# A tuned AdaLN attention block: new instruction orders on VectorE, ScalarE and GpSimd, weight pieces split in twos

## The reference, cut to what matters

```python
# x: 4 batches of 512 tokens, 512 wide; 32 query heads, 8 key/value heads, head width 128
h = layernorm(x) * (1 + ca) + sa
q = rope(h @ Wq.T)                               # 32 heads
c_kv = h @ Wdk.T
k = rope half of (h @ Wkr.T), other half (c_kv @ Wupk.T)
v = c_kv @ Wupv.T                                # 8 heads, each used by 4 query heads
p = softmax(causal(q @ k.T / sqrt(128)))
x = x + ga * ((p @ v) @ Wo.T)
h = layernorm(x) * (1 + cb) + sb
w = top-8 of softmax(h @ router.T + bias), others 0     # 64 experts
x = x + gb * (h * sum(w) + w @ expert_bias)
```

## Time and profile before

| | |
|---|---|
| Median of 3 runs | 1593.63 us (1592.9 to 1594.1) |
| The profiled execution's own time | 1594.98 us |
| Its span, first to last instruction | 1593.7 us |
| Busy: TensorE / VectorE / GpSimd / ScalarE | 93% / 74% / 67% / 61% |
| Granted TensorE clock, mean | 0.989 |

### The profile page before, as it was taken

One profiled execution on the slowest core, in us unless ns is written; L12 is line 12 of the kernel. 1 busy time (PEld: TensorE's weight loads), 2 busy tenths in 40 slices (PEclk: granted clock), 3 DMA queues, 4 the chain that ended last, 5 costly groups with the idle time before them and its releaser, 6 DMA issues.

```text
span 1593.7 us, 24295 instructions
## 1 busy us (share of the span) xinstructions
PE 1487.0 (93%) x7096; PEld 1223.8 (77%) x7096; DVE 1174.3 (74%) x3441; ACT 979.3 (61%) x2317; POOL 1063.5 (67%) x827
## 2 busy tenths in 40 slices
PE   7978999999999999999999999999899998899986
PEld 5567888888888888887888888888777777778864
DVE  6866777777777777777777777777787887788856
ACT  3256666666766666666667666666565555556663
POOL 1757766676665676666666567665676877786765
PEclk9999999999999999999999999999999999999997
DMA  8555665665765666566476566667687778677760
GB/s 306 204 177 178 220 189 178 183 202 174 208 205 169 196 202 192 181 195 198 160 216 200 166 206 203 193 187 225 190 245 219 253 219 261 217 234 253 235 215 27
DMA packets 210980, 321.99 MB, mean 202 GB/s; under 512 B 38416, under 2 KB 128272, under 8 KB 210848
## 3 DMA queue, kind: packets, MB, share of 16 engines
q1 hardware_dynamic: 210528, 320.33, 63.8%
q10 hardware_dynamic: 320, 0.11, 0.0%
HBM read 179.42 MB, written 140.94 MB: 201 GB/s over the span
## 4 chain that ended last, share of the span: by engine, by line
PE 45%; POOL 29%; DVE 10%; issue 5%; ACT 5%; DMA 4%; SPq 2%; DVEq 0%; POOLq 0%; ACTq 0%
PE bank_s L513 13%; POOL PT_lo L1551 13%; PE bank_o L613 10%; PE bank_pv L595 9%; PE bank_s L562 7%; PE bank_s L536 4%; DMA PT_raw<-blocks 3%; POOL qT_lo L1544 3%; POOL rot_c L1539 2%; POOL kT_lo L1560 2%; POOL kv_raw L1556 2%; ACT PT_hi L902 1%; DVE rot_s L1168 1%; DVE OT_lo L1231 1%; DVE rot_s L1169 1%
## 5 line engine op out<-in xcount | busy, mean ns | idle before, releaser
L1551 POOL TENSOR_TENSOR PT_lo<-PT_raw,PT_hi 128x640 fp32r<-128x640 f32 x252 | 393.7, 1586 | 47.5 <-ACT PT_hi L902 47.5
L888 ACT ACTIVATE probs<-probs,row_inv 128x512 f32<-128x512 f32 (+3 forms) x512 | 259.2, 555 | 252.2 <-DVE row_inv L1206 249.2
L1539 POOL TENSOR_TENSOR rot_c<-rot_c,rot_s 128x512 f32<-128x512 f32 x128 | 166.2, 1298 | 366.7 <-DVE rot_s L1169 366.5
L881 ACT ACTIVATE probs<-probs,row_min 128x512 f32<-128x512 f32 (+3 forms) x512 | 281.6, 552 | 120.8 <-DVE row_min L1200 120.8
L1200 DVE CUSTOM_DVE_ANT_0 probs<-bank_s,mask 128x512 f32<-128x512 f32 (+3 forms) x512 | 226.8, 487 | 2.3 <-issue 0.9
L562 PE MATMUL bank_s<-kT_lo,qT_hi 128*128 128x512 f32 (+3 forms) x512 | 165.2, 323 | 54.7 <-DVE kv_rot L1178 36.0
L1223 DVE STREAM_TRANSPOSE blocks<-probs 128x384 f32<-128x384 f32 x508 | 211.3, 445 | 3.6 <-POOL hT_lo L1529 2.1
L513 PE MATMUL bank_s<-hT_lo,wq_hi 128*128 128x512 f32 x500 | 201.5, 403 | 2.1 <-DVE row_min L1200 0.8
L613 PE MATMUL bank_o<-wo_lo,OT_hi 128*128 128x512 f32 x504 | 196.8, 391 | 2.9 <-DVE OT_lo L1231 2.9
L1544 POOL TENSOR_TENSOR qT_lo<-rot_c,qT_hi 128x512 fp32r<-128x512 f32 x128 | 167.3, 1307 | 46.8 <-ACT qT_hi L863 46.8
L613 PE MATMUL bank_o<-wo_hi,OT_lo 128*128 128x512 f32 x504 | 196.8, 390 | 0.0
(11 more groups left out here) (252 smaller groups left out, 3352.3 us busy)
## 6 DMA issues: line engine op xcount, KB each, us to landing
blocks<-blocks SPq DMA_DIRECT2D x127, 640.0 KB, 2.9
PT_raw<-blocks SPq DMA_DIRECT2D x504, 160.0 KB, 3.7
stage<-in_wq SPq DMA_DIRECT2D x32, 256.0 KB, 4.4
vblocks<-kv_raw SPq DMA_DIRECT2D x32, 256.0 KB, 4.0
kv_raw<-vblocks SPq DMA_DIRECT2D x128, 64.0 KB, 2.0
stage<-in_wo SPq DMA_DIRECT2D x32, 256.0 KB, 3.4
split_wq<-wq_hi SPq DMA_DIRECT2D x32, 256.0 KB, 4.1
split_wq<-wq_lo SPq DMA_DIRECT2D x32, 256.0 KB, 4.7
```

The costliest lines, as they stand in the source:

```text
L881: ins = act.activation(row(t, qt), row(t, qt), ACT.Exp, bias=row_min[m][:, qt:qt + 1], scale=-1.0, accum_out=row_sum[m][:, qt:qt + 1])
L888: ins = act.activation(row(t, qt), row(t, qt), ACT.Copy, scale=row_inv[t % 2][:, qt:qt + 1])
L1539: pool.tensor_tensor(rot_c[:], rot_c[:], rot_s[:], ALU.add).then_inc(pool_a, 1)
L1551: pool.tensor_tensor(lo[:, at], raw_of(t)[:, at], hi[:, at].bitcast(F32), ALU.subtract).then_inc(pool_t, 1)
```

## The change

**VectorE**: in h1 the low part of the values (`v_split_lo`) moves from behind `q_rope` and the second `invert_sums` to between the first `invert_sums` and `q_rope`. **ScalarE**: in h1 the high part of the values moves ahead of the second half of the exponentials; in h2 the high part of the keys moves from between the exponentials to between the two halves of `normalise`; the high part of the query made in an even step moves from that step's end to the next odd step's start, behind `pair_split_hi`. **GpSimd**: the low part of the query made in an even step moves likewise to the start of the odd step; the key's rotation moves from the end of h1 to h2, behind the low part of the probabilities, and the key's low part from before `q_rope` in h2 to after it; the FFN's pieces move (`ffn_gate` of a tile from two steps before its use to the start of the odd step in which VectorE uses it, `ffn_out` from the even step's end to the odd step's start). **Weights**: two pieces are split in every second step, in even steps only, and the order of the pieces changes; SyncE's loads and stores of them move into odd steps, and its store of a finished FFN tile (`store_out`) from the even step to the odd step. No instruction is added or removed.

```diff
--- before.py
+++ after.py
@@ -36,10 +36,11 @@
 LOWEST = -3e38
 
 
-CHUNKS = ["wo0", "wo1", "wo2", "wo3", "wk", "wq0", "wv", "wq1", "wq2", "wq3"]
-CHUNK_STEP = {1: [0], 2: [1], 3: [2], 4: [3], 5: [4], 6: [5], 7: [6], 8: [7], 9: [8], 10: [9]}
+CHUNKS = ["wo0", "wo1", "wo2", "wo3", "wk", "wq0", "wq1", "wq2", "wv", "wq3"]
+CHUNK_STEP = {2: [0, 1], 4: [2, 3], 6: [4, 5], 8: [6, 7], 10: [8, 9]}
 HALVES = [(3, 2), (1, 0)]
-FIRST_CHUNKS = CHUNKS[4:]
+
+FIRST_CHUNKS = ["wk", "wq0", "wv", "wq1", "wq2", "wq3"]
 FIRST = len(FIRST_CHUNKS)
 
 
@@ -497,6 +498,8 @@
                 g, b = place(u)
                 if u >= AGAIN:
                     pe.wait_ge(d_wl[name], 32 * (g + 1))
+                elif u == 0 and name in FIRST_CHUNKS:
+                    pe.wait_ge(pool_w, FIRST_CHUNKS.index(name) + 1)
                 elif b == 0:
                     i = CHUNKS.index(name)
                     pe.wait_ge(pool_w, chunk_event(g if i < 4 else g - 1, i) + 1)
@@ -968,24 +971,26 @@
                     pair_split_hi(t // 2 - 1, UPPER)
                 if h % 2 == 0 and t > 2:
                     pair_split_hi(t // 2 - 2, LOWER)
+                if h % 2 == 1 and t + 2 < ALL:
+                    q_split(t + 2)
                 if h % 2 == 0 and 0 < t < ALL - 2:
                     split_moved_hi(t - 1)
                 if n is not None:
                     ffn_exp(early(n - 3))
                 exponentials(t + 1, 0)
-                if h == 2 and u + 1 < UNITS:
-                    k_split(u + 1)
+                if h == 1:
+                    v_split_hi(u)
                 exponentials(t + 1, 1)
                 if t == ALL - 2:
                     split_moved_hi(t - 1)
-                if h == 1:
-                    v_split_hi(u)
                 normalise(t + 1, 0)
+                if h == 2 and u + 1 < UNITS:
+                    k_split(u + 1)
                 normalise(t + 1, 1)
                 if h % 2 == 1:
                     split_moved_hi(t - 1)
-                if t + 3 < ALL:
-                    q_split(t + 3)
+                    if t + 3 < ALL:
+                        q_split(t + 3)
                 for g, i in pieces(t):
                     split_chunk(g, i)
                 if t == FFN_FROM + 5:
@@ -1388,11 +1393,11 @@
                 if h == 3 and u > 0:
                     add_out(u - 1, LOWER)
                 invert_sums(t + 1, 0)
+                if h == 1:
+                    v_split_lo(u)
                 if t + 3 < ALL:
                     q_rope(t + 3)
                 invert_sums(t + 1, 1)
-                if h == 1:
-                    v_split_lo(u)
                 if h % 2 == 1:
                     transpose_blocks(t + 1, QUERY_ORDER[:2])
                 if h == 1 and u + 1 < UNITS:
@@ -1652,31 +1657,33 @@
 
             def step(t):
                 u, h, n, before = t // GROUP, t % GROUP, ffn_tile(t), ffn_tile(t - 1)
-                if h % 2 == 0 and t > 0:
+                if h % 2 == 1:
+                    if t + 2 < ALL:
+                        q_split(t + 2)
+                    if before is not None:
+                        ffn_gate(early(before))
+                        ffn_split_weights(early(before - 3))
+                        ffn_out(early(before - 4))
+                    if t + 3 < ALL:
+                        q_rope(t + 3)
                     split_moved_lo(t - 1)
-                if before is not None:
-                    ffn_split_weights(early(before - 3))
-                if n is not None:
-                    ffn_norm(early(n - 1))
-                if h == 2 and u + 1 < UNITS:
-                    k_split(u + 1)
-                if t + 3 < ALL:
-                    q_rope(t + 3)
-                if h % 2 == 1:
-                    split_moved_lo(t - 1)
-                if t + 3 < ALL:
-                    q_split(t + 3)
-                if h == 1 and u + 1 < UNITS:
-                    k_rope(u + 1)
+                    if t + 3 < ALL:
+                        q_split(t + 3)
+                    if before is not None:
+                        ffn_stats(early(before))
+                if h % 2 == 0:
+                    if t > 0:
+                        split_moved_lo(t - 1)
+                    if h == 2 and u + 1 < UNITS:
+                        k_rope(u + 1)
+                    if n is not None:
+                        ffn_norm(early(n - 1))
+                    if t + 3 < ALL:
+                        q_rope(t + 3)
+                    if h == 2 and u + 1 < UNITS:
+                        k_split(u + 1)
                 for g, i in pieces(t):
                     split_piece(CHUNKS[i], i % 2, chunk_event(g, i))
-                if n is not None:
-                    ffn_out(early(n - 4))
-                if before is not None:
-                    ffn_stats(early(before))
-                    ffn_gate(early(before + 1))
-                if t + 1 == FFN_FROM:
-                    ffn_gate(0)
                 if t == FFN_FROM + 5:
                     split_experts(0)
                 if t == ALL - 6:
@@ -1806,7 +1813,7 @@
 
             def store_split(g, i):
                 name = CHUNKS[i]
-                sp.wait_ge(pool_w, chunk_event(g, i) + 1)
+                sp.wait_ge(pool_w, chunk_event(g, i) + 1 if g >= 0 else FIRST)
                 for part, w in enumerate(chunk_target(name)):
                     sp.dma_start(split_d[name][g if i < 4 else g + 1, part], w.bitcast(F32)).then_inc(d_ws[name], 16)
 
@@ -1965,8 +1972,8 @@
                 for name, w in late:
                     load_split(name, w)
                 n, before = ffn_tile(t), ffn_tile(t - 1)
-                if n is not None:
-                    store_out(early(n - 4))
+                if before is not None:
+                    store_out(early(before - 4))
                 if before is not None and before + 1 < EARLY_TILES:
                     ffn_load(before + 1)
                 if t + 5 == FFN_FROM:
```

## The result

| | before | after |
|---|---|---|
| Median | 1593.87 us (1592.9 to 1595.18, 4 runs) | 1533.78 us (1533.06 to 1535.95, 4 runs) |
| Ratio to before, 95% interval | | 0.9625, 0.9608 to 0.9641 |
| Span of the profiled execution | 1593.7 us | 1532.8 us |
| Granted TensorE clock, mean | 0.989 | 0.983 |

The account below looks back on a forecast made before the run. TensorE, busy 93%, was taken as the bound at about 1487 us, so only its pauses could be won. Terms 1.5 + 36 + 8 + 2 = 47.5 us gave 1547.5 from the profiled 1594.98, 1546 from the median; range 1538 to 1570.

Parts of the forecast that it names:

- Two loops in a plain unit: Plain units: VectorE's loop and a hardly shorter GpSimd loop delay TensorE; the change wins 1.62 us a unit, 36 us.
- the new pause at h3: Plain units, h3's first scores: TensorE would wait 0.4 us for the key's low part.
- The DMA side: Weights in twos: reordering loads lose nothing, the store of blocks lands 1.9 us later, hidden; cost zero.
- h3's pause goes, since ScalarE loses its wait: Plain units, start of h3's product: moving the query's low part ends ScalarE's wait, winning 0.35 us per unit.
- Together 8 us: Steps 94 to 117 beside the FFN: 6 us over six units plus 2 from SyncE; bounds 0 and 16.
- The 1.1 us a unit that I named in brackets: Beside the FFN: 1.1 us more a unit if GpSimd left VectorE alone as in a plain unit.
- some 1: Beside the FFN: net win of some 1 us a unit, 6 us over six units.
- SyncE, 2 us forecast: Beside the FFN: store_out comes after the reordering loads that ScalarE waits for, winning two us.
- ScalarE's copy and OT_lo in h3, 1.3 forecast: Beside the FFN: h3 wins back 1.3 us of ScalarE's copy and of the output's low part.
- The bound of 16: Upper bound, 16 us, on the win beside the FFN, forecast at 8 us.
- Start and end: First h2 wins 1.5 us of its 3.82 us wait; two units behind the FFN win 1 us each.
- The order that I costed: GpSimd in h2: query rotation to 20.0, then key's low part to 21.25; h3 starts 1.27 us sooner.

Follow-up runs that it names:

- e1: Kernel before with only the values' high part (ScalarE) and low part (VectorE) moved; 1597.91 us, ratio 1.0008.
- e2: Changed kernel with only the values' high and low parts back at their old places; 1566.24 us, ratio 0.9812.
- e3: Changed kernel with the weight pieces converted one per step in their old order; 1560.26 us, ratio 0.9778.
- e7: Changed kernel with the odd heads' query high and low parts back at the end of the even step; 1531.13 us, ratio 0.9590.
- e4: Changed kernel with the key's low part back ahead of the query rotation on GpSimd in h2; 1523.83 us, ratio 0.9549.
- e10: Kernel before with only the values' parts moved and the weights in twos in the new order; 1577.41 us, ratio 0.9878.
- e5: Changed kernel with ffn_out on GpSimd and store_out on SyncE back in the even step; 1537.87 us, ratio 0.9636.
- e8: Changed kernel with the key's rotation on GpSimd back at the end of h1; 1536.78 us, ratio 0.9625.
- e9: Changed kernel with the key's low part ahead of GpSimd's query rotation and, beside the FFN, query and values' parts at old places; 1526.55 us, ratio 0.9566.
- e11: Changed kernel with the key's low part ahead of GpSimd's query rotation and, beside the FFN, the odd heads' query parts back; 1530.48 us, ratio 0.9589.

## Why the prediction was right or wrong

**Two loops in a plain unit: right, and shown.** e1, e2 and e3 each leave one loop closed: they win nothing, 0.4 and 0.5 us a unit, the change 1.7. The size was right too, 37.3 against 36. The terms moved a little: the low part of the values took 0.69, and the new pause at h3 is mostly 0.1 us or less instead of 0.4, but the h2 steps 10, 82 and 90 take 0.3, 0.5 and 2.0 us longer than their like (9.90). The DMA side held as well: the loads of PT_raw came no later (ScalarE starts on them at 9.12 from the start of h1, without a wait), and the store behind the six weight transfers, issued at 647.5, landed after 6.1 us, where I had allowed 4.8 + 1.9.

**"h3's pause goes, since ScalarE loses its wait": right in effect, half right in cause.** I gave it to the query's move. In a plain unit either move alone does it: e7 has only the key's, e4 only the query's. Without both, in e10, 1 us of pause is there.

**"Together 8 us" beside the FFN: the step that failed.** Measured are 16.7 us, or up to 23.5 without the half clock. The mis-sized term is VectorE's in h1: I charged the two instructions with two SBUF inputs 1.24 and 1.8 us, their length before; in step 101 they took 0.70 and 1.07, 1.27 us less, and the key rotation and then the key's low part, on which h3's start hangs, came sooner by about as much. So h1 and h2 together, 26.55 us in steps 101 and 102 before, didn't grow by 0.65 as I forecast; they fell by 0.62 (25.93). The 1.27 us stand in four of the six units. In the first two the sum took 0.69 us before as well, and the low part alone gives 1.1. Together that is 7.3 us. The 1.1 us a unit that I named in brackets and left out of the sum were right in size; GpSimd does not leave VectorE alone there, but what is left of its instruction is shorter.

The sum was also added up loosely. h3 starts 0.65 us later, counted from h1's start, so h1's own 0.9 is already in that, and with h3's 1.3 a unit wins 0.65, not "some 1": 3.9 + 2 = 5.9 us instead of 8. The other terms, from the lengths of the steps: SyncE, 2 us forecast; steps 110 and 112 fell from 16.82 and 14.54 to 14.35 and 11.62, which is 5.2 us beyond what their like changed, 3.2 more. ScalarE's copy and OT_lo in h3, 1.3 forecast; 12.98 became 11.28 where the clock stays up, 1.7, so 2.4 more in six units. And h0, which I gave nothing, fell from 12.08 to 11.62, some 2.6 in six units. With VectorE's 7.3 that makes 15.5 of the 17.6 us between 5.9 and 23.5; the last 2 I can't place. VectorE's share is read from the timelines, no run has it alone. The bound of 16 that I set was too low, even with the clock's 6.8 us taken off.

e5 and e8 each bring back 0.8 to 0.9 us in step 110, so the store and the sum don't explain the fall there alone. Which further move is needed with them wasn't tried.

**Start and end: mis-sized.** In step 2 the wait for kv_rot falls as forecast, from 3.82 to 2.08, and the scores of step 3 then wait 2.01 us for the key's low part. The clock took 1.7 us more than before in these steps, so nothing was won. At the end the two h2 steps, 118 and 122, won 1.41 us each where I said 1, and step 125 its wait of 1.92 for OT_lo, a gain of the query's move (e7) that I hadn't looked for.

**The clock: not in the prediction.** No term of it stands for the clock, so it was taken as unchanged.

**The order that I costed was not the best.** I costed the key's low part *behind* the rotation at 21.25 and 0.4 us of new pause, and didn't ask what one rotation less ahead of it would give: with the query's high part a step later, in a plain unit nobody waits for that rotation. e4 answers: 10 us, about half of it in the plain part.

## What to carry to other kernels

When two engines' chains between the same two points are about equally long, a move on one measures as nothing or little, and the two together win far more than each alone; try them in pairs before dropping either. In an in-order queue the thing to look for is not the busy share but which short instruction stands ahead of the one that TensorE waits for: one weight piece of 1.25 us on an engine busy 69% cost 1.2 us in every unit. And what a move is worth depends on the other orders around it, so after a good combination each part should be undone once; here one part of the change made it 10 us slower than it could be.

## What the runs showed of the hardware

**Two engines, one at a time.** The longer VectorE durations are not a slower rate. Of a VectorE instruction with two SBUF inputs that starts while GpSimd is in the middle of one, the time beyond some 0.55 us is the rest of GpSimd's instruction. Alone it takes 0.69. Three cases: 1.80 at 733.59, where GpSimd's rotation runs from 733.56 to 734.85 (1.26 left); 1.24 at 1227.92 beside a sum that ends at 1228.61 (0.69 left); 1.07 at 1187.56 beside a product that ends at 1188.08 (0.52 left). All low parts of the values that start so, in both kernels, fit within 0.02 us, down to one of 0.93 at 1384.51 with 0.38 left. It works in the other direction too. In this timeline of GpSimd, beside the two VectorE instructions of step 101 shown above, the small difference takes 0.65 us instead of 0.32, and the sum 1.63 instead of 1.30:

```profile
1186.18 0.65 POOL L1647 TENSOR_TENSOR weight<-rest,weight 128x64 fp32r<-128x64 f32 x1
1186.79 1.29 POOL L1654 TENSOR_TENSOR h<-h,gate 128x512 f32<-128x512 f32 x1
1188.16 1.63 POOL L1656 TENSOR_TENSOR h<-h,y 128x512 f32<-128x512 f32 x1
```

The Trainium skill (SBUF — State Buffer, "SBUF: two separate sides") says that the two share a port pair by an exclusive lock, held for a whole instruction, and that the other engine blocks. These cases agree with it. The price of such a move can therefore be worked out from the overlap that is left at its start, not from a typical length.

**A clock that falls after a pause, and not always.** In h3 of steps 103 and 111 of the changed kernel, 0.7 to 0.9 us behind a pause of 1.67 us at its start, TensorE's clock is granted at half for 3.4 us. In step 95 it falls 1.2 us ahead of h3, within a pause of 1.84 that follows one of 1.12, and stays down for 6.8 us. In steps 99, 107 and 115, after pauses of 1.84, 1.45 and 1.68, it doesn't fall. The steps with a fall take 12.8 to 13.8 us, the others 11.27 to 11.29. The windows of the trace (us, busy us and instructions of PE, PEld, DVE, ACT, POOL, granted clock, DMA share, GB/s) for the starts of steps 103 and 107:

```profile
1208.30:1211.70 3.40, 3.40 (x13) 3.11 (x13) 2.60 (x12) 2.25 (x8) 3.32 (x5) 0.51 0.21 87
1258.50:1261.90 3.40, 3.40 (x22) 3.05 (x21) 3.12 (x13) 2.29 (x8) 3.32 (x5) 1.00 0.31 127
```

0.51 is the lower of the two levels, 1.2 GHz; TensorE does 13 matmuls in the time of 22. All losses of the table's last column come in portions of about 1.7 us (3.4 us at half), sometimes two on end. The length of the pause does not decide. The kernel before has no fall beside the FFN, though it has pauses of 1.93 and 1.55 us in steps 110 and 112; e3 pauses 1.07 us at h3 in every plain unit and has none there. e4 and e9, with no pause over 0.61 at h3's start, have none beside the FFN, but e11 has the same 0.61 in steps 95 and 99, and there the clock falls 0.6 to 0.9 us behind it, for 6.8 us each time. Two of these rows of TensorE, of the kernel before (no fall) and of e11 (a fall):

```profile
1352.50 0.50 PE L595 MATMUL bank_pv<-PT_lo,v_hi 128*128 128x512 f32 x1 [1.93 <-POOL PT_lo L1551]
```

```profile
1151.23 0.47 PE L569 MATMUL bank_s<-kT_lo,qT_hi 128*128 128x512 f32 x1 [0.61 <-issue]
```

So a fall costs 1.7 to 3.4 us on top of the pause beside it, and what decides between the steps with and without a fall stays open. Of the 11.0 us between the profiled executions of the change and of e4, 6.8 are such falls beside the FFN.
